# A state-space layer: later rows' projections moved from the setup into six units, the second normalisation moved to ScalarE, first loads issued earlier

## What is computed

```
ada = silu(c) @ Wada.T + bada                     # shift, scale, gate, one row per batch
x_ssm = ln(x) * g1' + b1'                         # first normalisation, modulated
skip = x_ssm
x_ssm = ln(x_ssm, g2, b2)                         # second normalisation
mz = x_ssm @ Wz.T + bz ; act_mx = silu(x_ssm @ Wx.T + bx)
for d in (1, 2):                                  # direction 2 runs backwards in time
    z = mz @ Wc_d.T + bc_d
    dlt, Bm, Cm = split(z @ Wdbc_d.T)             # 64 + 16 + 16 numbers per token
    delta = softplus(dlt @ Wdt_d.T + bdt_d)
    h[t] = exp(delta * A) * h[t-1] + delta * Bm * z   # per channel e and state n
    y_d = sum over n of h * Cm + z * Dp_d
out = x + gate * ((act_mx * (y_1 + y_2)) @ Wf.T + bf + skip)
```

## Time and profile before

| | us |
|---|---|
| median of 3 runs | 3446.78 |
| lowest and highest | 3441.18, 3452.31 |
| the profiled execution, its own time | 3441.2 |
| its span | 3439.6 |
| its mean granted TensorE clock | 0.933 |

### The profile page before, as it was taken

How to read it: one execution, slowest core, us unless ns; L and a number is a source line. 1 busy time by engine, 2 the same in 40 slices (tenths; PEclk the granted TensorE clock), 3 DMA queues, 4 the chain that set the end, 5 groups by cost and what they waited for, 6 DMA issues and landing times.

```text
span 3439.6 us, 47915 instructions
## 1 busy us (share of the span) xinstructions
PE 2896.7 (84%) x16208; PEld 2088.2 (61%) x16208; DVE 3141.1 (91%) x2117; ACT 2628.9 (76%) x5032; POOL 3134.4 (91%) x1418
## 2 busy tenths in 40 slices
PE   8997788887778888888889888888889888888888
PEld 4654565666656665566666665666666665666665
DVE  1865999999999999999999999999999999999994
ACT  0225899887887899887777899987777898987772
POOL 0534999999999999999999999999999999999996
PEclk9998999999889999999999999999999999998999
DMA  5566443654456444644557344645557444644553
GB/s 208 199 219 230 148 154 132 221 194 160 148 193 245 133 154 158 246 152 165 186 196 258 131 157 152 250 151 165 182 202 255 131 160 152 246 154 163 183 194 120
DMA packets 224041, 623.12 MB, mean 181 GB/s; under 512 B 21980, under 2 KB 68252, under 8 KB 219960
## 3 DMA queue, kind: packets, MB, share of 16 engines
q1 hardware_dynamic: 221064, 599.11, 50.2%
q0 software_dynamic: 2592, 18.88, 1.6%
q10 hardware_dynamic: 144, 2.10, 0.2%
HBM read 539.75 MB, written 80.24 MB: 180 GB/s over the span
## 4 chain that ended last, share of the span: by engine, by line
POOL 33%; issue 23%; PE 21%; DVE 13%; ACT 1%; DMA 0%; POOLq 0%; DVEq 0%; SPq 0%; ACTq 0%
POOL dbu L1075 17%; POOL hbuf L1080 15%; DVE hbuf L1179 7%; PE y L797 7%; PE mb L770 6%; DVE slot L1179 4%; PE slot L808 3%; PE mb L844 1%; DVE du L1130 1%; PE mb L847 1%; DVE delta L1120 1%; PE mb L880 1%; PE slot L880 0%; PE y L880 0%; POOL skip L1086 0%
## 5 line engine op out<-in xcount | busy, mean ns | idle before, releaser
L1080 POOL TENSOR_TENSOR hbuf<-hbuf,cres 128x1024 f32<-128x1024 f32 x640 | 1508.1, 2373 | 33.6 <-DVE hbuf L1179 32.6
L1075 POOL TENSOR_TENSOR dbu<-bst,du 128x1024 f32<-128x1024 f32 x640 | 1506.9, 2373 | 34.5 <-DVE du L1130 22.5
L797 PE MATMUL y<-ident,hbuf 128*128 128x128 f32 x8192 | 1129.0, 289 | 295.3 <-POOL hbuf L1080 292.1
L797 PEld LDWEIGHTS y<-ident,hbuf 128*128 128x128 f32 x8192 | 997.2, 149 | 486.2 <-POOL hbuf L1080 384.7
L1001 ACT ACTIVATE abuf<-dut,bt 128x128 f32<-128x128 f32 x3072 | 971.0, 387 | 0.0
L1179 DVE TENSOR_TENSOR_SCAN hbuf<-dec,slot 128x1024 f32<-128x1024 f32 x384 | 874.6, 2278 | 41.8 <-PE slot L808 23.7
L1179 DVE TENSOR_TENSOR_SCAN slot<-slot,dbu 128x1024 f32<-128x1024 f32 x384 | 875.6, 2280 | 10.7 <-ACT slot L1039 5.3
L1039 ACT ACTIVATE slot<-delta,par 128x1024 f32<-128x1024 f32 x640 | 710.3, 1110 | 211.9 <-DVE hbuf L1184 198.5
L1179 DVE TENSOR_TENSOR_SCAN hbuf<-slot,dbu 128x1024 f32<-128x1024 f32 x256 | 580.5, 2268 | 1.7 <-ACT slot L1039 1.7
L808 PE MATMUL slot<-ident,abuf 128*128 128x128 f32 x3072 | 424.5, 283 | 178.7 <-ACT abuf L1001 170.7
L1039 ACT ACTIVATE dec<-delta,par 128x1024 f32<-128x1024 f32 x384 | 438.2, 1141 | 156.7 <-DVE hbuf L1179 156.7
(11 more groups left out here) (140 smaller groups left out, 2142.7 us busy)
## 6 DMA issues: line engine op xcount, KB each, us to landing
bst<-bc_s SPq DMA_DIRECT2D x640, 512.0 KB, 4.2
cres<-bc_s SPq DMA_DIRECT2D x128, 512.0 KB, 8.2
wzs<-wz_s SPq DMA_DIRECT2D x64, 256.0 KB
yf_s<-yrd SPq DMA_DIRECT2D x32, 512.0 KB, 5.4
ybuf<-yf_s SPq DMA_DIRECT2D x32, 512.0 KB, 5.8
yg_s<-ybuf SPq DMA_DIRECT2D x31, 512.0 KB, 2.9
si_s<-silu SPq DMA_DIRECT2D x28, 512.0 KB, 6.0
silu<-si_s SPq DMA_DIRECT2D x28, 512.0 KB, 4.5
```

Of the source, the lines that this page charges most:

```text
L797: last = nc.tensor.matmul(y[:, j * P:(j + 1) * P], hbuf[:, q % HR, j * P:(j + 1) * P], ident[:], start=False, stop=(q % N == N - 1), is_tr ...
L1075: nc.gpsimd.tensor_tensor(dbu[:, i % DR, :], bst[:, i % BR, :], du[:, k % 2, :], ALU.mult).then_inc(pool_b, 1)
L1080: nc.gpsimd.tensor_tensor(hbuf[:, q % HR, :], hbuf[:, q % HR, :], cres[:, q % N, :], ALU.mult).then_inc(pool_prod, 1)
```

## The change

- **Setup, projections.** Only blocks 0 and 1 (batch 0) are projected in the setup, in both directions: 4 projections in place of 16. wproj and the bias dbias go to HBM.
- **Units 9 to 14.** dbc_job(k) gives blocks 2 to 7. SP loads the block's tokens into the first half of wf at c = 7. TensorE projects for direction 1 into mb[0] at c = 15, for direction 2 into mb[1] at c = 0 of the next unit; ScalarE takes them out at c = 0 and c = 1; SP stores them at c = 5. wf itself is loaded at k = 16 and no longer at k = 8.
- **Second normalisation.** VectorE makes off = -mean * rs; ScalarE makes xn2 = rs * x + off by four Identity activations per block (normalised), one step before the block's transposes.
- **Steps.** FA is 2 and no longer 3, FX is 8 and no longer 9. The hardware loops over blocks become written-out ones, and the gain and shift are read from gs without a copy.
- **First loads.** The buffers and semaphores of unit 0's inputs belong to both blocks. The setup loads wzs and wdt of units 0 and 1 at f = 4, and dl, three bst buffers and the tokens at f = 12. In unit 0, z goes to the bank pair y and the transposed B to a slot, so that neither waits for delta to leave mb.

```
-        FA = 3
-        FX = NF + 1 - NC
+        FA = 2
+        FX = 8
+        FN = FX - 1
...
+            def load_first_products():
+                sp.wait_ge(dbo_out[0], 64)
+                sp.wait_ge(ones_ready, 1)
+                for h in range(2):
+                    sp.dma_start(dl[0:R, h * TC:(h + 1) * TC], scratch["dl"][0, h]).then_inc(dl_in, 16)
+                sp.dma_start(dl[R:R + N, :], scratch["bc"][0, 0, 0:N, :]).then_inc(dl_in, 16)
+                for i in range(BR):
+                    sp.dma_start(bst[:, i, :], scratch["bc"][0, 0, POOLED[i], :].partition_broadcast(P)).then_inc(b_in[i], 16)
...
+                if f == 4:
+                    load_first_units()
+                if f == FX + 4:
+                    load_first_products()
+                    for h in range(2):
+                        sp.wait_ge(xnt_first[h], 16 * DT)
+                        sp.dma_start(xn0[:, h], scratch["xn"][h]).then_inc(xn_in[h], 16)
...
+            for c in range(NC):
+                k = c % 2
+                for half in range(2):
+                    pool.wait_ge(ve_ready, 2 * c + half + 1)
+                    if half == 1 and c > 0:
+                        pool.wait_ge(n2_ready, TB * c)
+                    nc.gpsimd.tensor_tensor(rs[:, half, :], ve[:], mhalf[:], ALU.pow).then_inc(rs_ready, 1)
...
+                if c + 2 < NC:
                     pool.wait_ge(n2_ready, TB * (c + 1))
                     pool.dma_start(xin[:, k], t["x"][c + 2]).then_inc(x_in[k], 16)
...
+            def normalised(c):
+                act.wait_ge(off_ready, c + 1)
+                if c == 0:
+                    act.wait_ge(ada_mm, 3)
+                for j in range(TB):
+                    nc.scalar.activation(xn2[:, TB * c + j, :], xin[:, c % 2, j, :], ACT.Identity, scale=rs[:, 1, j:j + 1],
+                                         bias=off[:, j:j + 1]).then_inc(n2_ready, 1)
+
             for f in range(NF + 1):
-                if f >= FX:
+                if FN <= f < FN + NC:
+                    normalised(f - FN)
+                if FX <= f < FX + NC:
                     transposed_tokens(f - FX)
...
-                        for j in range(TB):
-                            nc.vector.tensor_scalar(xn2[:, bass.ds(TB * c + j, 1), :], xin[:, k, j, :], mv[:, j, 0:1],
-                                                    rs[:, j:j + 1], ALU.subtract, ALU.mult).then_inc(n2_ready, 1)
...
+                        nc.vector.scalar_tensor_tensor(out=off[:], in0=mv[:, :, 0], scalar=-1.0, in1=rs[:, 1, :],
+                                                       op0=ALU.mult, op1=ALU.mult).then_inc(off_ready, 1)
...
             pe.wait_ge(proj_ready[1], 2)
-            for c in range(NC):
+            for c in range(2):
...
+        def dbc_job(k):
+
+            return k - ET - 1 if ET < k < ET + 1 + NC - 2 else None
...
                     if k == ET and c == 0:
-                        sp.dma_start(wf[:], t["wfT"].rearrange("e p d -> p e d")).then_inc(wf_in, 16)
                         load_gate(0)
+                        sp.dma_start(wproj.rearrange("p a k r -> p (a k r)"), scratch["wproj"]).then_inc(pj_in, 16)
+                        sp.dma_start(dbias, scratch["dbias"]).then_inc(pj_in, 16)
+                    if k == 2 * ET and c == 0:
+                        sp.wait_ge(dbc_out, 64 * (NC - 2))
+                        sp.dma_start(wf[:], t["wfT"].rearrange("e p d -> p e d")).then_inc(wf_in, 16)
+                    if c == 5 and k > 0 and dbc_job(k - 1) is not None:
+                        store_dbc(dbc_job(k - 1))
+                    if c == 7 and dbc_job(k) is not None:
+                        if dbc_job(k) > 0:
+                            sp.wait_ge(dbc_mm, 2 * dbc_job(k))
+                        sp.dma_start(xc, scratch["xn"][dbc_job(k) + 2]).then_inc(xc_in, 16)
...
+            def make_dbc(j, d):
+                if d == 0:
+                    pe.wait_ge(xc_in, 16 * (j + 1))
+                    pe.wait_ge(pj_in, 32)
+                for i in range(DT):
+                    last = nc.tensor.matmul(mb[d][0:RD, :], wproj[:, d, i, :], xc[:, i, :],
+                                            start=(i == 0), stop=(i == DT - 1))
+                last.then_inc(dbc_mm, 1)
...
+                    if c == 0 and k > 0 and dbc_job(k - 1) is not None:
+                        pe.wait_ge(dut_ready, 2 * k + 2)
+                        make_dbc(dbc_job(k - 1), 1)
...
+                    if c in (0, 1) and k > 0 and dbc_job(k - 1) is not None:
+                        evict_dbc(dbc_job(k - 1), c)
```

185 lines of the change are left out of this document (112 added, 73 removed).

## The result

| | before | changed |
|---|---|---|
| median, us | 3452.31 (5 runs) | 3421.83 (5 runs) |
| lowest and highest | 3441.18, 3456.66 | 3421.17, 3423.44 |
| ratio, 95% interval | | 0.9926, 0.9906 to 0.9945 |
| profiled execution | 3441.2 | 3421.84 |
| its span | 3439.6 | 3419.9 |

A forecast was written before the change was run, and what follows sets the result against it. TensorE's sum was taken to bound the setup, GpSimd the units. Setup terms of -33.5 us, the units' start -7.9 and wf +1.5 made -39.9, taking the median from 3446.8 to 3407; range 3390 to 3424.

The forecast's parts named there:

- term 1: Setup: 12 of 16 projections leave TensorE, which has no gap, so all counts if tokens keep up; -41.5 us.
- the token chain: First rival, setup: VectorE and GpSimd hold each other up, or first loads delay folding weights; +10, 3417 us, chance 0.2.
- Units 9 to 14: Two added projection groups and two evictions per unit fit in existing waits; 0 us, bounds 0 and 7.
- Transposes between products: Setup: the last block's token transposes move between folding products instead of standing alone; -3.4 us.
- The copies: Setup: projections wait for VectorE's copy of wproj out of its bank; +1.7 us at f = 8, +0.7 in the tail.
- Second normalisation on ScalarE: Setup, f = 8 to 14: four activations delay the first ps[7] emptying, 0.8 us stall per step; +5.6, bounds 0.7 to 6.5.
- term 5: Setup, GpSimd's queue: rs behind a load makes an 8.9 us chain, fitting the step except at block 1; +1.8 us.
- The start of the units: Early loads and separate banks shorten the chain from second block to du from 22.96 to 15.0 us; -7.9, bounds -7 to -12.
- The rival's mechanism: Units 9 to 14: ScalarE's projection wait delays decays, stopping VectorE, then GpSimd; 50 us, 3459, chance 0.03.
- wf: Its 2 MB load moves from k = 8 (-1) to k = 16 (+2.5); +1.5 us, bounds -2 and +4.

## Why the prediction was half right

The sum was 22.4 us too good in the setup and right within 3 us elsewhere. The step that failed is term 1, "TensorE has no gap there, so all of it is on the path": 33.5 us were to leave the setup, and 11.1 did. In place of the missing ones the runs show a wait of 10.04 us for folding weights and a lower clock behind the bias products; with both taken away the forecast start of the units is nearly reached (282.8, forecast 281.0). That 3421.8 lies inside the range is luck as far as the cause goes: its upper part had been given to the token chain and to units 9 to 14. By the prediction's own steps:

1. *Projections out of the setup (-41.5).* The groups are gone, and their price was right: at 2.4 GHz two are 7.08 us. What failed is that all of it is on the path as long as the tokens keep up. A projection's 3.46 us had also covered for others: for the loads, for VectorE, and for the clock, which was 0.99 while a projection stood behind each 16 one-column products. From f = 8 on the terms make steps of 19.7, 16.2, five of 12.7, 11.9 and a tail of 9.0, in all 120.3. Measured from 118.71 on: 24.8, 16.05, 12.5, 13.6, 14.2 + 10.04 of wait, 13.8, 13.6, 13.6, 12.35, in all 144.6. Of the 24.3 us 10.0 are the wait for weights; 5.1 the step f = 8, 3 of them clock by the second profile of this kernel (21.7); 3.3 the tail (L399 and L420 are 2.7 above their full-clock times); 6.2 the steps f = 11 to 15, whose first four products take 1.1 to 1.9 us more than 1.88, less what the stalls stayed under the 0.8 counted. Against this stand 1.9 us: f = 8 began at 118.71, and by the sum it would have been 240.9 - 120.3 = 120.6.
2. *Transposes between products (-3.4).* Right: no group stands alone any more.
3. *The copies.* 1.7 forecast at f = 8, a wait of 1.27 measured; 0.7 in the tail, 0.80 measured.
4. *Second normalisation on ScalarE (+5.6).* L262 takes 2.92 us for four, 0.73 each; I had 0.78. Behind f = 8, whose wait belongs to term 5, the stalls are three of 0.3 to 0.5 us, 1.3 in all, and not seven of 0.8; within the bounds. The Trainium skill's figures (ScalarE: Activation LUTs, What ACT_TABLE_LOAD costs) gave the estimate of 2.9 for the four; the trace agrees to 0.02 us.
5. *GpSimd's queue (+1.8).* This step failed in its reasoning, though here it cost little, the wait of 3.22 us at f = 8 in place of 1.8 + 0.8; its steps of 14.7 us show once the other two losses are gone. 8.9 us was the chain from one normalisation to the next off; VectorE's whole block behind it is 14.7 (8.9 counted neither the first statistics nor L297 of the next block nor the long off, 1.22 beside GpSimd's L225 and 0.16 without). It was to be set against the step of 12.7, and was there to read: in before VectorE's L307 comes every 18.1 us, at 203.68 and 221.81, more than the step's 15.3:

```profile
203.68 5.59 DVE L307 TENSOR_SCALAR xn<-xin,mv,rs 128x512 f32 x4 [1.25 <-POOL rs L184]
```

   VectorE had been ahead by its early start only. The "10 us by which VectorE starts earlier" were no slack either: its second block waited until 114.20 for a normalisation that the list puts at f = 7.
6. *The start of the units (-7.9).* From the second block to du 14.7 us, forecast 15.0; delta of unit 1 is 8.7 us closer. The split between loads and banks was shown apart, 4.1 and 4.6. Right.
7. *Units 9 to 14 (0).* Right to 0.05 us a unit. The reason given, that two such groups fit at that boundary, holds: VectorE waits 0.17 us there. The rival's mechanism (ScalarE's wait for the projection holds back a decay, then VectorE and GpSimd stop) is real too: it is what the doubled groups show, from a second 3.5 us in a row on.
8. *wf (+1.5).* At k = 16 +3.6 us, over the 2.5 taken, in the bounds; at k = 8 and 9 the two units lost 1.8 and 2.9 us, 4.7 in place of 1. Together -1.2, where +1.5 was forecast. The units as a whole lost 0.6 us, since unit 1 took 1.7 us more, which is scatter (above).

Of the rivals the first came nearest, in its time (3417) and in its half sentence on the 3.7 MB ahead of the folding weights of f = 13, which is the wait of 10.04 us. It should have been a term: the rows gave the rate. Its other half, L297 slowed beside GpSimd's L189, did not come: L342, the same instruction, takes 2.73 us for four and starts as GpSimd's addition ends (125.88 against 121.00 + 4.94), so the pair wasn't seen. The Trainium skill (SBUF — State Buffer, Who interferes with whom) says that such a pair blocks each other; the small off (L353), which has two SBUF inputs and does stand beside L225, takes 1.22 us and not 0.16, and there the trace agrees. The other small instruction beside the addition, L339, takes 0.86 us in place of 0.17. And no chance was given to a lower clock in the setup, though a row on record had it. The sixteen folding products at 31.38 follow 16 one-column products without a gap and take 8.81 us (granted clock 0.59 from 31 to 34 us); the same sixteen take 7.11 elsewhere in that trace:

```profile
117.42 7.11 PE L393 MATMUL ps<-wz,wct 128*128 128x512 f32 x16
```

## What to carry to other kernels

When work is taken out of a loop in which several engines turn, compare each engine's whole period (start to start, waits for its own partners included) with the new step, not the chain behind one wait. A saving per step also takes away cover: from a load queue, whose next load must not stand behind megabytes that nobody needs yet, and from groups of one-column products, behind which TensorE here often ran at half clock for some 3 us; spreading those products between wide ones cost nothing here and gave 13.5 us. Idle time of an engine in a unit is no room for a long group: ask how long a group may be in the gap where it is put, and which engine's next work stands behind its result. Try combined edits together, since two reorderings that each gain can meet in one wait.
